# Two-layer graph attention and mixture stack: source rows reloaded from DRAM, gate bias on VectorE, combine transposes between two experts

## The reference, cut to what matters

```
Wh  = (h @ W.T + b).reshape(N, 4, 32)
src = einsum('nhd,hd->nh', Wh, a[:, :32]);  dst = einsum('nhd,hd->nh', Wh, a[:, 32:])
e   = leaky_relu(src[:, None, :] + dst[None, :, :], 0.2)
att = softmax(where(adj == 1, e, -9e15), axis=1);  x = x + einsum('ijh,jhd->ihd', att, Wh)

gate = x_normed @ Wg.T + bg                      # 2048 x 8
top2, idx = top_k(gate, 2);  combine = softmax(top2) placed at idx
out = sum over e of combine[:, e] * (relu(x_normed @ W1[e].T + b1[e]) @ W2[e].T + b2[e])
```

## Time and profile before

| | us |
|---|---|
| runs (3) | 662.14, 662.91, 664.7; median 662.91 |
| profiled execution | 663.44, its span 661.7 |
| PE busy | 568.8 (86% of the span) |
| DVE busy | 510.2 (77%) |
| ACT busy | 380.9 (58%) |
| POOL busy | 165.4 (25%) |
| mean granted TensorE clock | 0.936 |

### The profile page before, as it was taken

The page is one execution under the profiler, slowest core; times in us unless marked ns, Lnnn a source line. Parts: engine busy times, 40 slices in busy tenths (PEclk is TensorE's granted clock), DMA queues, the critical chain, the costliest instruction groups (busy, mean ns, idle before and its releaser), DMA issues.

```text
span 661.7 us, 13348 instructions
## 1 busy us (share of the span) xinstructions
PE 568.8 (86%) x5144; PEld 440.6 (67%) x5144; DVE 510.2 (77%) x900; ACT 380.9 (58%) x771; POOL 165.4 (25%) x186
## 2 busy tenths in 40 slices
PE   1878884999999999999998899989999745899985
PEld 1667874688776868866785584558789545467743
DVE  6699959795687667699939735997998998999520
ACT  1797792677876767784755727553421301565563
POOL 4300033021012100893522010030203000354741
PEclk9989795899998999998998899799999877799999
DMA  6475910021055055899498120020203824475750
GB/s 147 90 150 96 223 33 1 1 65 40 26 192 191 1 193 189 155 222 235 104 206 103 64 64 0 2 64 1 64 0 99 272 77 140 119 219 174 204 172 17
DMA packets 46372, 73.09 MB, mean 110 GB/s; under 512 B 4988, under 2 KB 24452, under 8 KB 46308
## 3 DMA queue, kind: packets, MB, share of 16 engines
q1 hardware_dynamic: 29956, 49.88, 24.2%
q0 software_dynamic: 15488, 22.02, 19.6%
q10 hardware_dynamic: 864, 0.33, 0.2%
HBM read 75.36 MB, written 22.02 MB: 147 GB/s over the span
## 4 chain that ended last, share of the span: by engine, by line
PE 61%; DVE 16%; ACT 13%; issue 5%; DMA 2%; POOL 1%; SPq 1%; ACTq 0%
PE bank L668 12%; PE bank L680 10%; PE bank L598 9%; DVE arena L1555 8%; PE bank L818 5%; ACT arena L1086 4%; PE bank L864 4%; PE bank L763 4%; PE bank L583 3%; PE bank L855 3%; ACT ysb L1043 2%; PE bank L779 2%; DVE arena L1389 2%; PE bank L547 1%; DMA routed_sums<-in_wsT 1%
## 5 line engine op out<-in xcount | busy, mean ns | idle before, releaser
L468 POOL TENSOR_TENSOR x<-x,ysb 128x512 f32<-128x512 f32 x36 | 70.2, 1950 | 262.9 <-ACT ysb L1043 261.7
L1086 ACT ACTIVATE arena<-heads,nd 128x512 bf16<-128x512 f32 x176 | 111.9, 720 | 20.3 <-PE bank L598 20.3
L668 PE MATMUL bank<-hTc,arena 128*128 128x512 f32 x192 | 95.6, 654 | 5.6 <-ACT reg_c L1032 5.6
L1555 DVE SCALAR_TENSOR_TENSOR arena<-reg_b,nd,arena 128x1536 f32<-128x1536 f32 x48 | 90.8, 1954 | 0.0
L680 PEld LDWEIGHTS bank<-arena,reg_c 128*128 128x128 f32 x768 | 87.5, 192 | 4.8 <-issue 4.8
L680 PE MATMUL bank<-arena,reg_c 128*128 128x128 f32 x768 | 87.8, 275 | 0.0
L1032 ACT ACTIVATE reg_c<-bank,b 128x512 f32<-128x512 f32 x96 | 65.3, 686 | 26.7 <-PE bank L668 26.7
L668 PEld LDWEIGHTS bank<-hTc,arena 128*128 128x128 f32 x192 | 39.5, 210 | 55.8 <-issue 47.3
L1043 ACT ACTIVATE ysb<-bank,comb 128x128 f32<-128x128 f32 x128 | 36.5, 367 | 63.1 <-PE bank L864 37.7
L598 PEld LDWEIGHTS bank<-reg_b,arena 128*128 128x128 bf16 x1536 | 70.8, 97 | 2.3 <-issue 1.7
L598 PE MATMUL bank<-reg_b,arena 128*128 128x99 bf16 x1536 | 71.8, 207 | 0.1
(11 more groups left out here) (187 smaller groups left out, 884.9 us busy)
## 6 DMA issues: line engine op xcount, KB each, us to landing
maskT<-routed_sums SPq DMA_DIRECT2D x48, 256.0 KB, 3.3
reg_c<-in_adj POOLq DMA_DIRECT2D x16, 512.0 KB, 6.8
arena<-in_w1T SPq DMA_DIRECT2D x16, 512.0 KB, 4.2
arena<-in_w2T SPq DMA_DIRECT2D x16, 512.0 KB, 5.4
routed_sums<-in_wsT SPq DMA_DIRECT2D x32, 256.0 KB, 5.4
routed_sums<-in_wrT POOLq DMA_DIRECT2D x32, 256.0 KB, 13.9
arena<-routed_sums SPq DMA_DIRECT2D x32, 256.0 KB, 3.1
routed_sums<-ident POOLq DMA_DIRECT2D x4, 1024.0 KB, 12.8
```

The lines of the kernel that those rows point to most:

```text
L468: nc.gpsimd.tensor_tensor(xi, xi, ysb[:, e % 3, :].rearrange("p (t d) -> p t d", d=P), ALU.add).then_inc(s_acc, 1)
L668: mm(bank[b][:, :], w1[:, s, e % 2, c * P:(c + 1) * P], hTc[:, :], start=True, stop=True).then_inc(full[b], 1)
L1086: last = af(ind[:, q, b, j, :], sbc[:, h, :], ACT.Relu, bias=nd[:, q * QT + j, h:h + 1], scale=BIG)
L1555: last = v.scalar_tensor_tensor(p, row, nd[:, t, h:h + 1], p if h else maskT[:, t, columns], ALU.max, ALU.mult)
```

## The change

- **Source rows.** At the start, PE makes for each of the chunks 1 to 3 one product whose stationary operand is only the 4 columns of source score weights (4 x 512 out), ACT copies the three results into the idle tile `hTc`, and SP stores them in a DRAM tensor `later_rows`. In `head(c, h)` ACT then issues, in place of copying a source row, a DMA that loads the row of 512 numbers broadcast to 128 partitions. PE makes no source row for chunks 1 to 3. DVE and ACT wait on `s_row[h]` before they read it.
- **Gate bias.** The bias is loaded in all 128 partitions and added by DVE at the head of `best`; the bias products are gone.
- **Combine transposes.** `combine_weights` (transposes and ACT's copy) stands between the two experts of the first pair; `combine` keeps the product.
- Counts of `bank7_full` and of source row events are adjusted.

```
+        later_rows = nc.dram_tensor("source_rows", (C - 1, H, CW), F32, kind="Internal").ap()
-            sp.dma_start(bg[:, :], a["bg"]).then_inc(s_w2, 16)
+            sp.dma_start(bg[:, :], a["bg"].to_broadcast([P, E0])).then_inc(s_w2, 16)
+            sp.wait_ge(ev["score"], C - 1)
+            for c in range(1, C):
+                sp.dma_start(later_rows[c - 1], hTc[(c - 1) * GRP:(c - 1) * GRP + H, :]).then_inc(s_spill, 16)
...
@@ PE, scores
-                    mm(o, hTc[:, i * P:(i + 1) * P], wgT[:, :], start=True, stop=False)
-                    last = mm(o, ones[0:1, :], bg[:, :], start=False, stop=True)
+                    last = mm(bank[4][:, i * E0:(i + 1) * E0], hTc[:, i * P:(i + 1) * P], wgT[:, :], start=True,
+                              stop=True)
@@ PE, second_layer
                     last.then_inc(full[b], 1)
+                    if e == 0:
+                        combine_weights()
@@ PE, start
             for h in range(H):
                 source_row(h, 0)
+            for c in range(1, C):
+                b = (0, 2, 4)[c - 1]
+                use(b, "score")
+                mm(bank[b][0:H, :], wxs[0][:, P:P + H], hT[:, bass.ts(c, CW)], start=True,
+                   stop=True).then_inc(full[b], 1)
@@ PE, chunk 0 and chunk0(c)
                 attend_first(h)
-                source_row(h, 1)
...
                     attend(h)
-                    source_row(h, c + 1)
@@ ACT, start
+            for c in range(1, C):
+                b = (0, 2, 4)[c - 1]
+                got(b)
+                last = af(hTc[(c - 1) * GRP:(c - 1) * GRP + H, :], bank[b][0:H, :], ACT.Copy)
+                last.then_inc(ev["score"], 1)
@@ ACT, head
                 if c < C - 1:
-                    source_row(h)
+                    act.wait_ge(s_spill, 16 * (C - 1))
+                    act.dma_start(sbc[:, h, :], later_rows[c, h:h + 1, :].to_broadcast([P, CW])).then_inc(s_row[h], 16)
@@ DVE, best
+                dve.wait_ge(s_w2, 16 * NW2)
+                then(v.tensor_tensor(sc[:, :, :], sc[:, :, :], bg[:, :].unsqueeze(1).to_broadcast([P, CT, E0]),
+                                     ALU.add))
```

More of the change, by code:

```diff
@@ L188, in gnn_moe_stack @@
         wgT = sb("wgT", [P, E0])
-        bg = sb("bg", [1, E0])
+        bg = sb("bg", [P, E0])
         b1 = sb("b1", [P, E0, HC])
@@ L223, in gnn_moe_stack @@
         s_adj = [sem(f"adj_slot{r}_loaded") for r in range(4)]
+        s_spill = sem("later_source_scores_stored")
+        s_row = [sem(f"source_row{h}_loaded") for h in range(H)]
         s_shared = sem("shared_weights_copied")
@@ L270, in gnn_moe_stack @@
             ("y", "weighted_output_ready"), ("htt", "hidden_tile_ready"),
-            ("bound", "weight_norms_ready"))}
+            ("bound", "weight_norms_ready"), ("score", "later_source_scores_ready"))}
         NW = 4 + 2 * H + 2
@@ L419, in load_rows @@
                 if r >= 4:
-                    pool.wait_ge(full[5 if r % 2 else 7], (r - 4) // 2 + 1 + (0 if r % 2 else 2 if r < 12 else 3))
+                    pool.wait_ge(full[5 if r % 2 else 7], (r - 4) // 2 + 1 + (0 if r % 2 else H // 2))
                 pool.dma_start(adj[:, r % 4, :], a["adj"][r * P:(r + 1) * P, :]).then_inc(s_adj[r % 4], 16)
@@ L641, in scores, with combine_weights @@
                 for i in range(CT):
-                    o = bank[4][:, i * E0:(i + 1) * E0]
-                    mm(o, hTc[:, i * P:(i + 1) * P], wgT[:, :], start=True, stop=False)
-                    last = mm(o, ones[0:1, :], bg[:, :], start=False, stop=True)
+                    last = mm(bank[4][:, i * E0:(i + 1) * E0], hTc[:, i * P:(i + 1) * P], wgT[:, :], start=True,
+                              stop=True)
                 last.then_inc(full[4], 1)
-            def combine(b=5):
+            def combine_weights():
                 pe.wait_ge(s_comb, k.event("comb"))
@@ L654, in combine @@
                 last.then_inc(full[6], 1)
+            def combine(b=5):
                 pe.wait_ge(ev["combT"], k.at("combT"))
@@ L1084, in above @@
                     act.wait_ge(full[1], user + 1)
+                if n >= H:
+                    act.wait_ge(s_row[h], 16 * (n // H))
                 for j in range(QT):
@@ L1410, in indicate @@
                     else:
-                        dve.wait_ge(ev["rows"], n + 1)
+                        if c:
+                            dve.wait_ge(s_row[h], 16 * c)
+                        else:
+                            dve.wait_ge(ev["rows"], n + 1)
                         dve.wait_ge(s_indf, (n - 1) * (Q - 1) + 1)
@@ L1589, in divisors @@
                 then(v.reciprocal(rden[:, 0:n], a3[:, 0:n, P]))
-            dve.wait_ge(ev["rows"], C * H + 3 * H)
+            dve.wait_ge(ev["rows"], H + 3 * H)
             wide_pair(0, range(2))
@@ L1601, in _ @@
                 wide_pair(g)
-            dve.wait_ge(ev["rows"], 2 * C * H)
+            dve.wait_ge(ev["rows"], H + C * H)
             dve.wait_ge(s_v1, C)
```

## The result

The changed kernel takes 657.11 us (median of 5 runs, 656.63 to 657.60) against 662.91 (5 runs beside them, 660.0 to 664.7): ratio 0.9922, 95% interval 0.9895 to 0.9949. The profiled execution is 657.6 us with a span of 655.8, against 663.44 and 661.7: 5.8 us less where 11.8 were forecast. The direction held; the time lies 5.9 us above the 651.2 forecast, 0.1 us outside the range of 646 to 657.

What follows compares the result with a forecast made beforehand. PE was taken as the bound, 61% of the chain that ended last. Terms +2.7 - 2.7 - 5.7 - 3.9 - 1.3 + 0.2 (second attention) + 0.1 - 1.2 = -11.8 us gave 651.2 us, range 646 to 657.

Steps and rivals of the forecast that it cites:

- Start, +2.7: At the start: three new 4 x 512 products take 2.66 us while DVE waits, so all of chunk 0 moves 2.7 us.
- rival 3: Start and chunk 0: the start's 2.7 us aren't paid back, giving 654 us; chance 0.13.
- Chunk 0, -2.7: Chunk 0: PE's 5.28 us wait for ACT's row copy and ACT's 2.62 us idle time go, saving 2.7 us.
- Chunk 1, -5.7: Chunk 1: gate bias 2.1 us, rows of heads 2 to 4 2.8 us, first head 0.8 us saved.
- rival 6: Chunks 1 to 3: gate bias products were nearly free, giving 0.6 us for 4.6; 655 us; chance 0.03.
- Chunk 2, -3.9: Chunk 2: gate bias 1.26 us, first head 0.8, second and fourth 0.93 each saved; third head's row worth nothing.
- Chunk 3, -1.3: Chunk 3: only the gate bias is saved, 4 x 0.31 us; there are no rows.
- Combine, +0.1: Combine transposes between experts: the move gives between -0.5 and +0.3 us, taken as +0.1.
- Clock, -1.2: Starts of chunks 2 and 3: fewer small products avoid half of 1.7 + 0.7 us lost to clock falls.
- Rival 4: Chunks 1 and 2: ACT sets the pace, about 5.2 us less gain, 656.5 us; chance 0.12.
- rival 5: ACT's twelve load issues stall it at 2.9 us each, not 0.45, making the kernel slower, 675 us; chance 0.05.
- Rival 2: Both clock falls go and the clock rises earlier in chunk 1 too, giving 648 us; chance 0.15.

Runs made afterwards that it cites:

- scores_behind_bound: Changed kernel with the start's three 4 x 512 products moved behind the score bound's product, ACT's copies behind the exponentials; 654.45 us, 0.9895 to before.
- bias_only: Kernel before with only the gate bias moved to an addition on DVE; 654.61 us, 0.9919 to before.
- combine_only: Kernel before with only the combine transposes and ACT's copy of them moved between the first two experts; 660.76 us, 1.0010 to before.
- no_combine_move: Changed kernel with the combine transposes and their copy put back beside the product; 658.01 us, 0.9944 to before.
- after_again: Changed kernel run again with no edit; 657.87 us, 0.9969 to before.
- filler_chunk0: Changed kernel with unread 512-column products behind the sums of the four heads of chunk 0 alone; 657.63 us, 0.9931 to before.
- no_loads_chunk2: Changed kernel without the four source row loads ACT issues in chunk 2 (result left wrong, only time read); 657.93 us, 0.9931 to before.
- bias_filler_end0: bias_only with six unread 512-column products at the end of chunk 0; 650.92 us, 0.9847 to before.
- bias_filler8_gap: bias_filler_end0 with eight unread products for six, plus one ahead of the experts' bias product in chunks 1 and 2; 654.26 us, 0.9902 to before.
- rows_only: Kernel before with only the source rows stored in DRAM and loaded back; 663.19 us, 1.0050 to before.
- rows_start_late: rows_only with the start's three products and copies moved behind the bound and the exponentials; 661.48 us, 1.0007 to before.
- filler_all: Changed kernel with an unread 512-column product behind the sums of every head of chunks 0 to 2; 661.23 us, 0.9977 to before.
- filler_end0: Changed kernel with ten unread 512-column products at the end of chunk 0; 654.68 us, 0.9917 to before.

## Where the prediction was right and where it was wrong

- **Start, +2.7.** The products took 2.68. Counted right; DVE began 3.5 us later, 0.7 of it not from these products. That chunk 0 would pay it back was right in net (-0.6 against 0), and it could have been avoided, which the run `scores_behind_bound` shows: rival 3 fell.
- **Chunk 0, -2.7.** The mechanism was right (5.28 gone, the wait at bank 2, ACT's idle time gone), the size too small: about -4.
- **Chunk 1, -5.7.** The time fell by 3.7, since a low stretch came in the second head's sums (1.5 us), and the 2.1 us of bias products, priced at half clock, gave 0.5 of it back to the first layer behind them. Gate bias: `bias_only` gains 4.7 us by its median and 5.3 by its ratio for terms of 4.7, so rival 6 fell.
- **Chunk 2, -3.9.** This is where most was lost: +2.6. I said "the copies are released by PE's earlier work, so what was saved before is kept". The copies were released 6.0 us earlier (248.99 for 255.03), but the last landed 1.6 us slower, as one of the rows' own loads ran beside it, ACT then waited for POOL, and 6.8 us at the low clock began in PE's wait, 2.6 us of the chain. The section on the loads asked only if they come late, not what they do to other transfers.
- **Chunk 3, -1.3.** Gate bias as forecast (-1.3 without the clock); up to 5.1 of the gain of 6.4 is clock.
- **Combine, +0.1**: `combine_only` and `no_combine_move` both show no effect; one under some 2 us can't be excluded.
- **Clock, -1.2.** This is the step that failed, in sign: 1.2 us were to come back, and in chunks 1 and 2 the low clock took up to 6.2 more than before. I weighed only the two falls that the trace showed, and which the change might avoid, and not the ones that it might bring. Nor did the two go: in the five profiles of the changed kernel and its nearest relatives (`after_again`, `no_combine_move`, `filler_chunk0`, `no_loads_chunk2`), the one at the start of chunk 2 is there five times and the one at the start of chunk 3 three times. The idea behind the term was not empty: with the bias on DVE and the rows kept (`bias_only`, `bias_filler_end0`, `bias_filler8_gap`) one of these six places is low, with the bias on PE (before, `combine_only`, `rows_only`, `rows_start_late`) all eight. With the rows gone as well they are mostly back. A reading that fits, argued and not shown: a wait of PE that ACT, DVE or a DMA sets stays as long while PE's work around it shrinks.
- **What the clock of the runs says.** The median clock of before is 0.943 to 0.951 in four groups, 0.946 of `combine_only`, 0.930 to 0.931 of the two kernels with rows alone, 0.933 to 0.934 of the changed kernel; unread products put back raised it to 0.938 to 0.948. That the profiled runs of before and after both show 0.936 hid it: 0.936 is the low end of what before was granted in the other groups. Of that pair's shortfall of 5.9 us the clock is thus up to 3.7 (2.5 taken behind chunk 0; the 1.2 of the forecast not given back); the rest is what the DRAM chain added in chunk 2, the price of the bias products in chunk 1 and the last stage, less what chunk 0 made up.
- **Swings of the clock.** The Trainium skill describes them in "TensorE: Matmul & The Clock Gate", section "A second HAM failure mode: psum-queue depth-cycling": where PE idles briefly and often between groups of products, the clock swings between its two levels, and this costs throughput. This case's traces agree in part: the same sums took 7.46 us behind an open wait of 1.3 us and 5.92 behind a filled one, but also 5.92 behind an open one in before and in `scores_behind_bound`.
- **Rival 4**, ACT as pace setter, gave 656.5, nearest to the time, but for another reason: in chunk 1 of the changed kernel ACT is busy 64.92 of 90.4 us and PE 88.31. ACT's issues took 0.33 to 0.35 each, so rival 5 fell. Rival 2, both falls gone and the clock up earlier in chunk 1, fell: the low stretch that runs into chunk 1 ends at 117.4 us for 119.3, and the falls are the ones told above.

What stays open: why the loss of the rows brings low stretches, and which of the falls beyond 290 us come from what. They differ between executions of one program (275 us in one profile of the changed kernel, 295 and 370 us in the other), and no run here controls them. The low stretch by the DRAM chain is not in every execution: in the second profile chunk 2 took 93.0 us (199.39 to 292.34), not 95.2. (The prediction's sum leads to 651.1 us; its 651.2 is a rounding.)

## What to carry to other kernels

When a trace shows a clock that drops, the length of the work that leaves PE is only an upper bound of what it gives: here 10.6 us of forecast work gave 6 us or less, and six useless products in an idle stretch gave about 5 (`bias_filler_end0` against `bias_only`, in different groups; their intervals just touch). Compare the clock over several runs of both kernels, not in two profiles. Products that can go into a wait are worth a try beside products to remove, and each such try is to be measured: of the eight kernels here with unread products, three (`filler_all`, `filler_chunk0`, `bias_filler8_gap`) gained nothing by them. A broadcast load that is itself hidden can still lengthen a DMA that the chain waits for, here by 0.5 to 1.5 us.

## What the runs showed of the hardware

- A product with 4 stationary columns and 512 moving ones in float32 cost 0.89 us in the changed kernel (2.68 for three), as one with 128 stationary columns did (0.885).
- The same wait of PE ahead of the experts' bias product in chunk 1 (1.24 us before, 1.32 in the changed kernel) is followed by the full clock before and by a low stretch in both profiles of the changed kernel; in the run `filler_end0` that stretch is missing in chunk 1 and there in chunk 2, and in `scores_behind_bound` it is missing in both.
- A broadcast load of 256 KB, issued by ACT in 0.33 to 0.35 us, went with a landing of 7.2 to 8.2 us of the 256 KB DRAM-to-DRAM copy that it ran beside (eleven profiles); without it the copy took 6.61 (before) and 6.71 us (`no_loads_chunk2`).
- Over 62 runs of before, the time rose by 0.47 us for each microsecond of span x (1 - clock), over 28 runs of the changed kernel and its nearest relatives by 0.50: about half of the most that the low clock could cost.
